# Four projections of a six-layer attention stack as three float32r products each, with the weights kept as high and low parts and refilled in pieces of 256 columns

## The reference, cut to what matters

```python
def attn_layer(x, Wqkv, qs, ksc, Wo):        # 16 heads of 64, window of 32 tokens
    q, k, v = split(x @ Wqkv, 3)             # Wqkv is 128 x 3072
    q, k = l2norm(q) * qs, l2norm(k) * ksc
    q, k = rotary(q), rotary(k)              # tables with a scale per position
    return local_attention(q, k, v) @ Wo     # softmax over this window and the one before
def ffn_layer(x, g, bln, W1, b1, W2, b2):
    xn = (x - mean) / sqrt(var + 1e-05) * g + bln
    a, gate = split(xn @ W1 + b1, 2)         # W1 is 128 x 682, halves of 341
    return a * gelu(gate) @ W2 + b2
for i in range(6):
    x = attn_layer(shift_tokens(x), ...) + x
    x = ffn_layer(shift_tokens(x), ...) + x
```

## Time and profile before

| | |
|---|---|
| median of the runs | 4271.77 us (4268.67 to 4274.26) |
| profiled execution, its own time | 4290.08 us |
| its span, first to last instruction | 4288.3 us |
| instructions in the trace | 142841 |
| mean granted TensorE clock | 0.959 |
| TensorE busy | 3861.1 us (90%) |
| VectorE busy | 2766.0 us (65%) |
| GpSimd busy | 2315.8 us (54%) |
| ScalarE busy | 1754.0 us (41%) |

### The profile page before, as it was taken

How to read it: one execution, slowest core, us unless ns; L and a number is a source line. 1 busy time by engine, 2 the same in 40 slices (tenths; PEclk the granted TensorE clock), 3 DMA queues, 4 the chain that set the end, 5 groups by cost and what they waited for, 6 DMA issues and landing times.

```text
span 4288.3 us, 142841 instructions
## 1 busy us (share of the span) xinstructions
PE 3861.1 (90%) x63688; PEld 2066.3 (48%) x63880; DVE 2766.0 (65%) x3583; ACT 1754.0 (41%) x2815; POOL 2315.8 (54%) x1774
## 2 busy tenths in 40 slices
PE   8999997788999899998899998999999899999887
PEld 4444443344454445454444454444454444454444
DVE  4554553666677677676677676677776666676662
ACT  4545553334344434343333343434343433343333
POOL 0000000766776666676666666666676666666651
PEclk9999998899999999999999999999999999999997
DMA  1000000554444544444444445444454344444431
GB/s 44 6 6 6 8 3 20 157 162 132 132 140 135 159 135 135 135 145 128 155 135 135 135 138 156 135 135 135 137 174 133 119 135 134 135 140 133 131 118 42
DMA packets 206787, 489.95 MB, mean 114 GB/s; under 512 B 62558, under 2 KB 85340, under 8 KB 205276
## 3 DMA queue, kind: packets, MB, share of 16 engines
q1 hardware_dynamic: 196080, 465.08, 34.7%
q10 hardware_dynamic: 10092, 15.73, 1.1%
HBM read 224.80 MB, written 7.34 MB: 54 GB/s over the span
## 4 chain that ended last, share of the span: by engine, by line
PE 67%; DVE 11%; issue 10%; ACT 9%; DMA 2%; POOL 1%; SPq 0%; ACTq 0%; DVEq 0%; POOLq 0%
PE PS L498 67%; ACT AOT L1163 3%; DVE MX L932 3%; ACT SX L1140 2%; DVE TPB L906 2%; DMA PP<-PX 2%; ACT SC L1157 1%; DVE SC L934 1%; DVE PP L950 1%; DVE PX L951 1%; ACT PA L1094 1%; DVE AO L871 0%; ACT VV L1153 0%; DVE VAR L972 0%; DVE VAR L970 0%
## 5 line engine op out<-in xcount | busy, mean ns | idle before, releaser
L906 DVE SCALAR_TENSOR_TENSOR TPB<-PS,VEC,C 128x1024 f32<-128x1024 f32 x768 | 984.4, 1283 | 621.9 <-ACT SX L1140 602.8
L498 PE MATMUL PS<-X,W 128*128 128x512 f32 x1536 | 854.2, 640 | 4.4 <-issue 2.4
L498 PEld LDWEIGHTS PS<-PP,VV 32*64 32x64 f32 x24576 | 444.8, 134 | 666.8 <-issue 636.9
L1243 POOL TENSOR_TENSOR SC<-SC,RC 128x1024 f32<-128x1024 f32 x192 | 365.5, 1904 | 703.1 <-DVE RC L943 702.8
L498 PE MATMUL PS<-PP,VV 32*64 32x64 f32 (+1 forms) x24576 | 552.3, 224 | 210.4 <-ACT AOT L1163 125.5
L1230 POOL TENSOR_TENSOR Q<-Q,RB 128x512 f32<-128x512 f32 x384 | 487.8, 1270 | 295.2 <-DMA RB<-root_scratch 294.3
L1140 ACT ACTIVATE SX<-PS 128x512 f32<-128x512 f32 x768 | 461.4, 601 | 364.9 <-PE PS L498 364.9
L1238 POOL TENSOR_TENSOR Q<-TPB,TR 128x512 f32<-128x512 f32 x384 | 489.1, 1274 | 130.2 <-DMA TR<-TPB 120.4
L1153 ACT COPY VV<-PS 128x512 f32<-128x512 f32 x384 | 223.6, 582 | 753.7 <-PE PS L498 753.7
L1238 POOL TENSOR_TENSOR K<-TPB,TR 128x512 f32<-128x512 f32 x384 | 489.3, 1274 | 0.0
L1230 POOL TENSOR_TENSOR K<-K,RB 128x512 f32<-128x512 f32 x384 | 488.6, 1272 | 0.0
(11 more groups left out here) (144 smaller groups left out, 4933.7 us busy)
## 6 DMA issues: line engine op xcount, KB each, us to landing
TR<-TPB SPq DMA_DIRECT2D x768, 256.0 KB
RB<-root_scratch SPq DMA_DIRECT2D x768, 256.0 KB, 4.0
PP<-PX SPq DMA_DIRECT2D x192, 192.0 KB, 2.6
W<-in_wqkv ACTq DMA_DIRECT2D x6, 1536.0 KB, 10.3
PP<-PX SPq DMA_DIRECT2D x192, 48.0 KB, 2.3
root_scratch<-NV SPq DMA_DIRECT2D x384, 8.0 KB, 1.4
WO<-in_wo ACTq DMA_DIRECT2D x6, 512.0 KB, 11.3
T<-in_x SPq DMA_DIRECT2D x8, 256.0 KB, 3.1
```

The source lines that it names most:

```text
L498: return e.matmul(dst, lhsT, rhs, start=start, stop=stop, **kw)
L906: e.scalar_tensor_tensor(TPB[:, n % 3:4 + n % 2:3 + n % 2 - n % 3, w, :], g, VEC[:, l, 9 + w:10 + w], C[:, at:at + 1024].rearrange("p (o c ...
L1243: e.tensor_tensor(sc, sc, RC[m % 2][:, :].rearrange("p (g o) -> p g o", o=1).broadcast_to([128, 16, 64]), ALU.mult).then_inc(sem["np_pool" ...
```

## The change

- Q, K, V and W1 products are done by `mm3`: high part times high part, high times low, low times high, in float32r. The weights are kept as `LH`/`LL` and `W1H`/`W1L`, the inputs as `LX` (high and low, two buffers) and `XCH`/`XCL`.
- To make these parts, ScalarE casts (high part) and GpSimd subtracts (low part): once a unit for the projections' input (stage `XS`, at the start of phase 7), once a unit for the input of F4 (stage `F3`), 12 times a layer for a piece of 256 columns of Wqkv (stage `WC`), and once a layer for W1 (stage `W1`).
- Each layer weight exists once. The pieces of Wqkv go through three small buffers `WS` (stage `LW`, a DMA that ScalarE issues) and are cast behind the last use of their columns by the layer before.
- F4 is split into 128, 128 and 85 hidden features (before: 114, 114 and 113), and its products are 128 columns wide.
- `PX` has one buffer where it had two.

The diff, cut to its core:

```diff
-FP = [(0, 114), (114, 114), (228, 113)]
+FP = [(0, 128), (128, 128), (256, 85)]
...
+    for l in range(DEPTH):
+        first = 64 * l
+        at = [first - 13 + c for c in range(8)] + [first - 5, first - 4, first - 1, first]
+        if l == 0:
+            at = [-8, -8, -8, -7, -7, -6, -6, -5, -5, -4, -4, -3]
+        for c in range(3):
+            do(at[0] - 2 if l else -9, o.put, "LW", 12 * l + c)
+        for c in range(12):
+            do(at[c], o.put, "WC", 12 * l + c)
+            if c < 9:
+                do(at[c], o.put, "LW", 12 * l + c + 3)
+        do(first + 1, o.put, "L1", l)
+        do(first + 3, group, "WB", l, "wb_dve", l + 1)
+        do(first + 9, o.put, "W1", l)
...
+    for u in range(NB * DEPTH):
+        do(8 * u - 9, o.put, "XS", u)
...
TensorE
-                    mm(bk(st, key)[:, :], W[l % 2][:, c], X[:, b, 0:L]).then_inc(sem["pj_pe"], 1)
+                    mm3(bk(st, key)[:, :], LH[:, c], LL[:, c], xh[:, :], xl[:, :]).then_inc(sem["pj_pe"], 1)
...
-                    mm(bk(st, key)[0:n, :], W1[l % 2][:, at:at + n], XC[:, :]).then_inc(sem["f4_pe"], 1)
+                    on.wait_ge("xc_pool", u + 1)
+                    mm3(bk(st, key)[:, :], W1H[:, w, c], W1L[:, w, c], XCH[:, :], XCL[:, :]).then_inc(sem["f4_pe"], 1)
...
ScalarE
+                if st == "LW":
+                    else:
+                        on.wait_ge("wc_pool", i - 2)
+                    e.dma_start(dst, src).then_inc(sem[f"ws_in{i % 3}"], 16)
...
+                elif st == "WC":
+                    on.wait_ge(f"ws_in{i % 3}", 16 * (i // 3) + 16)
+                    e.copy(dst, src).then_inc(sem["wc_act"], 1)
...
+                elif st == "XS":
+                    e.copy(LX[u % 2][0][:, :], X[:, u % NB, 0:L]).then_inc(sem["xs_act"], 1)
+                elif st == "F3":
+                    on.wait_ge("f3_dve", u + 1)
+                    e.copy(XCH[:, :], H[2][:, :]).then_inc(sem["xc_act"], 1)
...
GpSimd
+                elif st == "WC":
+                    on.wait_ge("wc_act", i + 1)
+                    e.tensor_tensor(lo, src, hi.bitcast(F32), ALU.subtract).then_inc(sem["wc_pool"], 1)
...
+                elif st == "XS":
+                    on.wait_ge("xs_act", u + 1)
+                    e.tensor_tensor(xl[:, :], X[:, b, 0:L], xh[:, :].bitcast(F32), ALU.subtract).then_inc(sem["xs_pool"], 1)
+                elif st == "F3":
+                    on.wait_ge("xc_act", u + 1)
+                    e.tensor_tensor(XCL[:, :], H[2][:, :], XCH[:, :].bitcast(F32), ALU.subtract).then_inc(sem["xc_pool"], 1)
```

More of the change, by code:

```diff
@@ L240, in fill, with do @@
             group("F5", u, "f5_dve", 2 * u + 2)
[L242 to L249, removed]
+    turn = {}
+    def do(n, f, *a):
+        turn.setdefault(n, []).append(lambda: f(*a))
+    for l in range(DEPTH):
[12 more added lines that the diff above has]
+        do(first + 9, o.put, "W1", l)
+        do(first + 4 if l else -9, o.put, "LO", l)
+        do(first + 9 if l else -9, o.put, "L2", l)
+    for u in range(NB * DEPTH):
+        do(8 * u - 9, o.put, "XS", u)
     vp = {7: (1, 0), 0: (0, 1), 1: (0, 2), 2: (0, 3), 3: (0, 4), 4: (0, 5), 5: (0, 6), 6: (0, 7)}
-    for n in range(-8, NS + 9):
+    for n in range(-9, NS + 9):
         u, k, m, p = n // 8, n % 8, n // 2, (n - 3) // 2
@@ L255, in order @@
         ss = 0 <= n + 7 < NS
[L256 to L259, removed]
+        for f in turn.get(n, ()):
+            f()
         if even and scores:
@@ L347, in build @@
             KA = sb("KA", [128, 6, L], F32R, ca)
[L348 to L351, removed]
+        LH = sb("LH", [128, 3072], F32R)
+        LL = sb("LL", [128, 3072], F32R)
+        WS = sb("WS", [128, 3, 256])
+        W1s = WS[:, :, :].rearrange("p a c -> p (a c)")[:, 0:2 * F1]
+        LO = sb("LO", [128, 8, 128])
+        W1H = sb("W1H", [128, 2, 384], F32R)
+        W1L = sb("W1L", [128, 2, 384], F32R)
+        W2 = sb("W2", [128, 3, 128])
+        LX = [(sb(f"LXH{i}", [128, L], F32R), sb(f"LXL{i}", [128, L], F32R)) for i in range(2)]
         BI = [sb(f"BI{i}", [128, 8]) for i in range(2)]
@@ L362, in build @@
         PP = [sb(f"PP{i}", [128, 2, 16, 32]) for i in range(2)]
-        PX = [sb(f"PX{i}", [128, 16, 32]) for i in range(2)]
+        PX = sb("PX", [128, 16, 32])
         MX = sb("MX", [128, 16])
@@ L368, in build @@
         RB = [sb(f"RB{i}", [128, 2, L]) for i in range(2)]
-        XC = sb("XC", [128, L])
+        XCH = sb("XCH", [128, L], F32R)
+        XCL = sb("XCL", [128, L], F32R)
         H = [sb(f"H{i}", [128, L]) for i in range(3)]
@@ L720, in tensor_program @@
                     for hp in range(8):
-                        p = mm(bk(st, key)[:, :], WO[l % 2][:, hp, :], AOT[:, hp, :], hp == 0, hp == 7)
+                        p = mm(bk(st, key)[:, :], LO[:, hp, :], AOT[:, hp, :], hp == 0, hp == 7)
                     p.then_inc(sem["wo_pe"], 1)
@@ L1031, in scalar_program @@
[L1031 to L1033 removed]
+                    elif c < 3:
+                        on.wait_ge("w1_pool", l)
+                    else:
+                        on.wait_ge("wc_pool", i - 2)
+                    if c < 8:
+                        src = wqkv[l][:, 0:2048].rearrange("p (w c) -> p w c", w=2)[:, :, 128 * c:128 * c + 128]
+                        dst = WS[:, i % 3, :].rearrange("p (w c) -> p w c", w=2)
+                    else:
+                        src, dst = wqkv[l][:, 256 * c:256 * c + 256], WS[:, i % 3, :]
@@ L1170, in scalar_program @@
                     e.activation(H[0][:, :], bk(st, key)[:, :], ACT.Square).then_inc(sem["f1_act"], 1)
-                    e.copy(XC[:, :], bk(st, key)[:, :]).then_inc(sem["f1_act"], 1)
+                    e.copy(H[1][:, :], bk(st, key)[:, :]).then_inc(sem["f1_act"], 1)
                 elif st == "F2":
```

131 lines of the change are left out of this document (89 added, 42 removed).

## The result

The changed kernel took 4391.95 us in the median (4387.02 to 4393.95, four runs); the kernel before, on the same chip, 4273.02 us (4268.67 to 4293.95, four runs). The ratio is 1.0267, with a 95% interval of 1.0232 to 1.0301: slower by 2.7%, or 119 us, where 146 us were forecast. The time lies in the stated range of 4175 to 4490 us.

What follows compares the result with a forecast made beforehand. It took TensorE's work as the bound, except in even slots of phases 2, 4 and 6, set by the route through AOT. Units +139, boundaries +12 and start -5 gave +146 us on 4271.77: 4418 us, range 4175 to 4490.

Steps and rivals of the forecast that it cites:

- The hold: Phase 7: GpSimd's subtractions, waiting for input, delay the softmax multiplication 4.1 us and F4; +2.9 us a unit.
- The clock: Behind the F4 stall and AOT waits of phases 2, 4, 6: lower TensorE clock, +1.0 and +0.4 us a unit.
- The products: Q, K, V and F4 products: 0.16 us saved each, -1.4 us a unit, nothing in phases 2, 4, 6.
- rival 3: Everywhere: AOT waits shrink with the products too, full gain of 4.8 us a unit, 4042 us; chance 0.04.
- Layer boundaries: Five layer boundaries: weight casts, subtractions and ScalarE's wait add 2.5 us each, 12 us together, bounds 0 and 30.
- The start: Start of the layers: loading a small weight piece first lets the first product begin earlier, -5 us.
- rival 5: GpSimd or ScalarE fills up: lateness not caught up by phase 1 is paid again, +270 us, 4540 us; chance 0.06.
- Rival 2: F4: TensorE's work decides and the hold is hidden, -1.9 us a unit, -91 us, 4180 us; chance 0.20.

Runs made afterwards that it cites:

- e1: Changed kernel, but VectorE computes XCL and the XS cast and subtraction stand at the end of phase 7: 4240.87 us, ratio 0.9899.
- e2: Changed kernel with only the two XS steps moved to the end of phase 7, XCL staying on GpSimd: 4346.18 us, ratio 1.013.
- e4: Kernel before, float32 products, plus an unused ScalarE cast and two unused GpSimd subtractions where the changed kernel has its own: 4415.69 us, ratio 1.0305.
- e3: Changed kernel with ten bf16 products of 256 columns put ahead of F4's fifth product: 4372.28 us, ratio 1.0208.
- e7: Changed kernel with the layers from the second on reusing the Q, K and V pieces of layer 0: 4348.38 us, ratio 1.0156.
- e9: Kernel of e8 with the DMA of the next weight piece issued one slot later: 4191.78 us, ratio 0.9795.
- e6: Changed kernel with only the high times high product of each mm3, all casts and subtractions kept: 4279.23 us, ratio 0.9994.
- e11: Kernel of e9 with a piece's cast and subtraction moved from the slot's start to behind its softmax multiplication: 4230.62 us, ratio 0.9886.
- e8: Kernel of e1 with the V products of phases 1, 3 and 5 moved into the even slots behind them: 4201.69 us, ratio 0.9814.

## Why the prediction was right

- **The hold** (forecast +2.9 us a unit, 4.1 us late at the softmax multiplication): shown. From the end of `H<-H,PS`, 2159.90, to the start of the softmax multiplication, 2165.59, it takes 5.7 us, where 5.8 was forecast. TensorE waits for H 48 times, 3.26 us in the phase shown and 2.7 us in the mean, for "some 3 us". e1, e2 and e4 take the hold away, halve it and add it alone. With its clock it costs 130 us (e4) to 157 us (e1 against after). That is 2.7 to 3.3 us a unit, where 2.9 and 1.0 of clock, 3.9 together, were forecast.
- **The clock** (forecast +1.0 behind the F4 stall, +0.4 behind the AOT waits): the direction is right, 0.959 to 0.934. What the first costs in time was not measured by itself: e3, which fills less than half of the stall, gives back 0.5 us a unit, and e4 loses 0.004 of clock. The span times what is missing to a clock of 1 was 176 us before, 290 us after and 238 us in e1. So 52 us of lost clock, 1.1 us a unit, go with the hold, and the other 62 us are there without it. I had tied the clock to the stall and the AOT waits. Not all of this lost clock lengthens the kernel, since other engines set the pace in many slots.
- **The products** (forecast -1.4 us a unit, 0.16 each): two `mm3` take 1.58 us in the layers, against 1.60 forecast and 1.92 before. By the Trainium skill ("FP8 and Floating Point Precision", section "TensorE Precision Notes"), true float32 takes four passes through the array; three passes for each product would make the two an estimated 1.44 us, and the trace does not bear out this estimate, here either. The wait for AOT grew from 125.5 to 149.0 us, and phases 2 and 3 are not shorter at all, so rival 3 is out. Phases 0 and 1 gained 1.0 where I took 0.5, phases 4 and 5 gained 0.3, and phases 2 and 3 nothing, where I took 0.9 for phases 3 and 5 together. All that is neither hold nor refill nor start is 119 - 130 - 47 - 2 = -60 us by e4, and -87 us with e1's price of the hold. The forecast had -1.4 + 0.4, or -48 us. This is a remainder, and the intervals of its terms leave it open within some 30 us.
- **Layer boundaries** (forecast +12 us, bounds 0 and 30): mis-sized. e7 gives 47 us, above the bounds, though its own interval (24 to 70 us) reaches into them. I had priced the piece in phase 7 and taken ScalarE's waits as covered; e9 shows that these are a small part too. Where the rest goes is in part open.
- **The start** (forecast -5 us): the first product of the layers does come 6.5 us behind the first weight DMA instead of 9.85 us, but the first mark of an even slot comes 1.5 us later than before (785.2 against 783.7). The pieces behind the first take it back: at 764.94 TensorE has waited 5.58 us for a square of ScalarE, which itself stood 5.02 us for GpSimd's LL of the first layer's refill. It is the kind of wait that the refill also has at the layer boundaries.
- **GpSimd's amount of work** (rival 5): 2491.9 - 2315.8 = 176 us more, against 180 forecast, and no second lateness; e1, with only 41 us less of it, loses nothing.
- **Rival 2** (TensorE's work decides) is refuted by e6: with 453 us less TensorE work the 48 waits grew.

The forecast came out 27 us high. That it came so near is in part luck: by e4's price the hold with its clock was forecast 57 us too high, the boundaries 35 us and the start 7 us too low, the rest 12 us too high, and these errors partly cancel. The mechanism is shown, the size of the sum's terms only roughly.

Here are the two timeline rows of the start, with the first weight DMA and the product that answers to the earlier trace rows:

```profile
741.67 1.48 ACTq L1052 DMA_DIRECT2D WS<-in_wqkv  x3
...
748.12 0.80 PE L518 MATMUL PS<-LXH,LH 128*128 128x512 f32 x1 [7.99 <-POOL LL L1309]
```

**What stays open.** By which way some 40 us of the refill's 47 come about, and whether VectorE's long instructions on the norms are what makes e11 slower than e9. In e9 the 60 casts and subtractions from the second layer on still stand at the slots' starts. That they are paid there by their amount was only argued.

## What to carry to other kernels

When a step moves to an engine with room, look at what stands behind it in that engine's queue: a wait of 2.9 us there held work that was ready, and a subtraction of 1.28 us behind it was paid about one to one, though GpSimd was busy 57% of the time. A gain on the engine with the largest busy share is worth something only in stretches where that engine waits for nobody. Where a stretch ends in a wait for another engine, moving work into it can be worth more than making the work cheaper: 1.3% by order alone here, 0.8% by the cheaper products. Look at the other engines' waits afterwards: in e8 only a third of the filled wait was gained.

## What the runs showed of the hardware

**Less work on TensorE, and a lower clock.** In e6 TensorE had 578 us less work than in the kernel before and was granted a mean clock of 0.849 in place of 0.959. The span in 40 slices of e6:

```profile
PEclk9999998687888888888888878888888887888886
```

The clock is below 0.9 in every slice of the layers, where the kernel before is below it only in the first and the last of them. The same instructions take longer there: a product of PP and VV takes 246 ns, against 230 in the kernel after and 225 in the earlier trace rows.

```profile
L518 PE MATMUL PS<-PP,VV 32*64 32x64 f32 x23040 | 637.0, 246 | 430.8 <-DMA PP<-PX 176.9 <-ACT AOT L1235 153.8 <-issue 99.1
```

It also waits 176.9 us for the DMA from PX, which is 28.2 us in the kernel after. So part of what is saved on TensorE is lost to the clock.

**Stalls that end with nothing the profile shows.** TensorE is idle for up to 5.4 us at a time with "issue" as the only reason, 83 such waits of 122.3 us in the kernel before. One of them, in the sums of squares of a phase 0:

```profile
2069.36 1.06 PE L498 MATMUL PS<-SX,C 128*32 128x128 f32 x11 [5.02 <-issue]
```

The phases 0 and 1 of that unit took 21.8 us, where the median of all units is 14.1. Such waits grew to 148.5 us after. What causes them no run here shows.
